# Windowed attention of a fused network on one Trainium2 core: in the last lane of a layer, the turn of a pair moved ahead of the values of the pair before it

## The reference, cut to what matters

```python
DIM, DEPTH, HEADS, DIM_HEAD, WINDOW = 128, 2, 8, 64, 64   # B, N = 2, 1024
def _layer(x, wqkv, qs, ksc, wo, lg, lb, w1, b1, w2, b2):
    h = shift_token(x)
    q, k, v = heads of h @ wqkv
    q, k = l2norm(q) * qs, l2norm(k) * ksc
    q, k = rotary_xpos(q, k)
    o = local_attention(q, k, v)      # each 64 tokens see themselves and the 64 before
    x = x + o @ wo
    h = layer_norm(shift_token(x)) * lg + lb
    a, g = split(h @ w1 + b1)
    return x + (a * gelu(g)) @ w2 + b2
```

## Time and profile before

| | |
|---|---|
| runs of the kernel | 2834.72, 2840.59, 2842.88 us, median 2840.59 |
| the profiled execution | 2833.55 us, its span 2831.8 us |
| mean granted clock of PE in it | 0.978 |
| busy share of the span | PE 94%, DVE 68%, ACT 66%, POOL 37% |
| windowed attention, last lanes | near 1920, 2153, 2522 and 2752 us of the span |

### The profile page before, as it was taken

One profiled execution on the slowest core, in us unless ns is written; L12 is line 12 of the kernel. 1 busy time (PEld: TensorE's weight loads), 2 busy tenths in 40 slices (PEclk: granted clock), 3 DMA queues, 4 the chain that ended last, 5 costly groups with the idle time before them and its releaser, 6 DMA issues.

```text
span 2831.8 us, 63348 instructions
## 1 busy us (share of the span) xinstructions
PE 2659.5 (94%) x24036; PEld 1812.7 (64%) x24036; DVE 1939.5 (68%) x5616; ACT 1858.8 (66%) x4392; POOL 1051.8 (37%) x876
## 2 busy tenths in 40 slices
PE   8999999999999998899999998998898998998998
PEld 5666656548888885588888885455455563553554
DVE  5555646488788786788888886774675326764774
ACT  5666766626676673478787876776776515875875
POOL 2323323313333330355555552553454013552551
PEclk8999999999999998999999999999999999999999
DMA  1010000000000001000000002210210002111210
GB/s 56 1 43 1 13 1 9 5 9 2 3 2 2 2 2 50 30 2 2 2 2 2 2 2 92 62 45 7 61 49 20 24 1 69 47 30 30 49 42 16
DMA packets 35280, 63.13 MB, mean 22 GB/s; under 512 B 11526, under 2 KB 15654, under 8 KB 33830
## 3 DMA queue, kind: packets, MB, share of 16 engines
q1 hardware_dynamic: 34982, 59.07, 7.5%
HBM read 23.48 MB, written 1.15 MB: 9 GB/s over the span
## 4 chain that ended last, share of the span: by engine, by line
PE 73%; DVE 11%; ACT 7%; issue 3%; SPq 2%; POOL 1%; DMA 1%; DVEq 0%; ACTq 0%; POOLq 0%
PE bank L804 63%; PE bank L1033 5%; PE bank L1153 3%; SPq L770 2%; PE bank L880 1%; ACT low L1364 1%; DVE low L1708 1%; DVE low L1686 1%; ACT work L1400 1%; ACT work L1303 1%; DVE halves L1701 1%; DMA work<-work 1%; DVE work L1588 1%; ACT squared L1275 1%; ACT bank L1279 1%
## 5 line engine op out<-in xcount | busy, mean ns | idle before, releaser
L1271 ACT ACTIVATE low<-bank 128x512 f32<-128x512 f32 (+3 forms) x512 | 427.8, 946 | 0.0
L804 PE MATMUL bank<-table_keys,halves 128*128 128x512 f32 (+3 forms) x1536 | 418.0, 380 | 1.1 <-ACT low L1364 1.0
L804 PE MATMUL bank<-work 128*64 128x128 f32 (+6 forms) x4480 | 364.2, 290 | 39.7 <-DVE work L1795 20.7
L804 PEld LDWEIGHTS bank<-work 128*64 128x64 f32 (+3 forms) x4480 | 265.0, 144 | 211.5 <-issue 147.5
L1364 ACT ACTIVATE low<-bank,low 128x512 f32<-128x512 f32 (+23 forms) x384 | 227.2, 592 | 248.9 <-DVE low L1708 245.4
L1708 DVE TENSOR_REDUCE low<-bank 128x1 f32<-128x512 f32 (+22 forms) x512 | 286.4, 569 | 96.2 <-PE bank L804 91.3
L1898 POOL TENSOR_TENSOR halves<-squared,const 128x512 fp32r<-128x512 f32 x128 | 137.0, 1070 | 510.7 <-PE bank L804 510.7
L1271 ACT ACTIVATE work<-bank 128x512 f32<-128x512 f32 (+4 forms) x389 | 199.5, 538 | 151.2 <-PE bank L804 76.9
L804 PEld LDWEIGHTS bank<-table_keys,halves 128*128 128x128 f32 x1536 | 243.6, 190 | 47.6 <-issue 13.3
L1400 ACT ACTIVATE work<-work 128x192 f32<-128x192 f32 (+1 forms) x512 | 218.7, 431 | 38.2 <-DVE work L1788 38.2
L1947 POOL TENSOR_TENSOR work<-work 128x768 f32<-128x768 f32 x128 | 187.7, 1466 | 135.2 <-DVE work L1799 135.2
(11 more groups left out here) (201 smaller groups left out, 5707.3 us busy)
## 6 DMA issues: line engine op xcount, KB each, us to landing
work<-work SPq DMA_DIRECT2D x512, 64.0 KB, 2.0
slot<-in_wW SPq DMA_DIRECT2D x4, 1605.5 KB, 6.7
slot<-in_wA SPq DMA_DIRECT2D x4, 837.0 KB, 6.4
table_low<-embv_padded SPq DMA_DIRECT2D x2, 1536.0 KB, 6.3
table<-in_dft SPq DMA_DIRECT2D x1, 3072.0 KB, 11.8
slot<-in_wE SPq DMA_DIRECT2D x2, 584.0 KB, 3.7
const<-in_const SPq DMA_DIRECT2D x1, 1094.5 KB, 5.2
squared<-in_x SPq DMA_DIRECT2D x4, 256.0 KB, 6.2
```

Source lines behind the costliest of these rows:

```text
L804: return pe.matmul(o, l, r, start=start, stop=stop)
L1271: return act.activation(dst, src, ACT.Identity)
```

## The change

In iterations of the last lane but its first, and after them (`turned`), the step `w_turn` of pair j - 1 is added behind `w_exps` and ahead of the values of pair j - 2, and not at its old place behind `w_weigh`. This holds for j = 25 to 31. Iteration 32 has `at` = 0 and keeps the old order (values 30, turn 31). Nothing else moves.

```diff
@@ -377,6 +377,10 @@
                     rotate(r)
                 if j < len(pairs):
                     add("w_exps", c=lane, i=i, hp=hp)
+                turned = (c >= C - 1 and at > 0)
+                if turned and j <= len(pairs):
+                    lane, i, hp = pairs[j - 1]
+                    add("w_turn", c=lane, i=i, hp=hp)
                 if 2 <= j <= len(pairs) + 1:
                     lane, i, hp = pairs[j - 2]
                     if i == 0:
@@ -393,7 +397,7 @@
                     add("w_weigh", c=lane, i=i, hp=hp)
                 if c + 1 < C and at in (3, 4, 5, 6):
                     add("w_value", c=c + 1, i=at - 3)
-                if 1 <= j <= len(pairs):
+                if not turned and 1 <= j <= len(pairs):
                     lane, i, hp = pairs[j - 1]
                     add("w_turn", c=lane, i=i, hp=hp)
                 if c and at == 2:
```

## The result

The changed kernel takes 2864.66 us (median of 5 runs, 2858.76 to 2867.73), the kernel before 2842.88 in the same comparison: ratio 1.0078, 95% interval 1.0053 to 1.0104, 21.8 us more. The forecast was 2856.5, 15.9 more, in a range of 2845 to 2868. The change is slower, for the reason forecast. Both medians lie above the sum of 15.9, and both intervals still hold it. In the profiled execution the schedule makes 17.2 us, and most of what it has beyond this is the clock.

A forecast was written before the change was run, and what follows sets the result against it. The prediction took latency, a chain of waits through several engines, to bound the last lanes. 2.35 + 0.81 + 0.81 = 3.97 us a lane, +15.9 in four, on the median 2840.59 gave 2856.5 us, range 2845 to 2868.

The forecast's parts named there:

- DVE's wait: On DVE, the turned tile's copy passes the next reciprocal, which then waits for PE's turn; reciprocal 25 at 2756.42, not 2754.95.
- Rival A: DVE's wait in iterations 25 and 26 is absorbed; only values 26 and 28 add, +6.5 us, 2847.1; chance 0.09.
- Rival B: Earlier copies remove PE's waits ahead of values 24, 26, 28: -7.0 us, 2830.9 with both clock falls gone; chance 0.05.
- Rival D: Engine order is not the plan's, so nothing moves: 2840.6 us; chance 0.03.
- Iterations 25 and 26: From turn 24 to lane 2's output product, reciprocal and turn 25 come later: +2.35 us a lane.
- Iterations 27 to 30: From scores 27 to scores 31, values 26 and 28 come onto the chain, 0.81 each: +1.6 us a lane.
- V26 0.81: Values 26 on PE, now between turn 27 and the norm's mean, adds 0.81 us from scores 27 to 29.
- Iteration 31 to V31: From scores 31 to values 31 at the lane's end: stays 8.21 us, 0 added; values 30 starts 0.3 us earlier.
- I keep two falls, as now: PE's clock falls to half in two of the four last lanes, as before, at 1.37 us each.
- a sign of being wrong: In the changed trace, a half clock showing in more than two last lanes would count against the forecast.
- Rival C: PE's clock falls in new gaps: every lane +2.7 us, 2859.2; one more in each +5.5, 2862.0; chance 0.13.

The follow-up runs named there:

- e1: The changed kernel with DVE back in the old order, new order kept on PE and ACT: 2852.79 us, 1.0045 of the kernel before.
- e9: The kernel before with the new order on DVE alone and 16 filler transposes ahead of values 30: 2837.28 us, 0.9971 of the kernel before.
- e4: The changed kernel with the change kept in iterations 27 to 31 alone: 2847.70 us, 1.0029 of the kernel before.
- e3: The changed kernel with the change kept in iterations 25 and 26 alone: 2846.74 us, 1.0030 of the kernel before.
- e8: The changed kernel run again, unaltered, on another chip: 2856.36 us against 2837.10 of the kernel before, 1.0066.
- e5: The changed kernel with PE's idle places filled by useless transposes of the identity: 2847.21 us, 1.0031 of the kernel before.
- e6: The kernel before with 18 useless transposes filling PE's gap ahead of values 30: 2831.28 us, 0.9976 of the kernel before.
- e7: The kernel before with the norm of lane 2 moved into PE's waits: 2821.19 us, 0.9933 of the kernel before.
- e11: The kernel before with 18 transposes ahead of values 30, repeated on another chip: 2829.12 us, 0.9944 of the kernel before.

## Why the prediction was right, and where its sum was short

*Direction and mechanism.* Right. DVE's wait: T24 at 2.58 us and its copy 0.91 us later, as forecast; the reciprocal behind it, the turn behind that. e1 takes the DVE half away and gets reciprocal 25 back, e9 has it alone. PE's half: S27 to S31 grows in e1 and e4 and not in e3 or e9. Rival A (the reciprocal keeps up) falls with the earlier trace rows against the DVE rows of after. Rival B (the copies free PE) too: the waits of 0.80 us ahead of V26 and V28 did go, and gave nothing, since T27 and T29 wait for POOL anyway. Rival D falls with the order of the rows.

*Iterations 25 and 26: +2.35 forecast, 2.21 measured* (8.31 - 6.10), and 2.31 up to S27. I had added the full lengths of copy and scaling, 0.69 and 0.68; back to back they start 0.61 and 0.60 apart. After it the product takes 3.63 us to S27 instead of 3.53.

*Iterations 27 to 30: +1.62 forecast, 1.99 to 2.00 measured.* The term "V26 0.81" was right, and its neighbours grew: T27 to V26 is 1.02 us, where a turn ahead of the 512-column matmuls of the norm took 0.93; the norm to S29 is 1.05, where it was 0.95. 0.19 a step, two steps.

*Iteration 31 to V31: 0 forecast; 0 at a full clock* (8.21 in the first lane of e8, 8.20 to 8.22 in e5). V30 starts 0.56 us earlier, where 0.3 was forecast, and gains nothing, since T31 waits for the multiply.

Together 4.30 us a lane and 17.2 in all against 3.97 and 15.9; between the two filled kernels the runs give 15.9. That this is the forecast's own number is luck, since those intervals reach over 3 us to either side. So is the match of e8's 2856.36 with the 2856.5: the kernel before stood 3.5 us lower there than the median that I added to.

*The clock: this is the term that failed.* "I keep two falls, as now", at 1.37 us each. The first profile after has a half clock in every last lane, which I had named as a sign of being wrong. In two of them there is a second, earlier fall, in T24, V23 and S26 of the second and in V26, the norm and S29 of the third. And a fall is dearer than the one I priced, because it lasts longer. Before, the granted clock was back by V31; now, in three of the four lanes, it stays at 0.50 through T31 and V31 and into the product. Windows behind T31 of the first lane before, and in the product of the fourth after (columns as in the earlier trace rows):

```profile
1953.40:1954.00 0.60, 0.00 (x0) 0.00 (x0) 0.60 (x1) 0.00 (x0) 0.00 (x0) 1.00 0.00 0
...
2818.00:2820.00 2.00, 2.00 (x3) 0.67 (x2) 0.00 (x0) 0.00 (x0) 0.00 (x0) 0.50 0.00 0
```

By windows of half a microsecond the first of these falls lasts from 1949.7 to 1953.2, some 3.4 us, and costs 1.37; the second from 2810.6 to 2820.9, 10.2 us, and costs 3.9 (45.54 against 41.65). The step that went wrong was to judge each new gap by itself, by V22 behind 1.45 us, and to price every fall by the shortest kind. What makes a fall long stays open: it isn't the shorter gap ahead of V30, since e1 and e3, whose gap there is 2.54 us as before, have falls of 10 us and more too.

Rival C had the direction and, for this profile, the count: six falls where there were two, one more a lane. Its price for one was too low by a factor of up to three. Between the medians of the runs, though, the clock adds only some 3.4 us (e5, e6, e8), less than C's 5.5, and that isn't clear of noise: the first profiled execution of the changed kernel was one of its slower ones, and e8's, at 2856.79 us, has three falls, in the second, third and fourth lane.

The Trainium skill ("TensorE: Matmul & The Clock Gate", Part 1) says that activity releases the throttle and that the point of the transition varies, because the activity is watched in a free-running way. The traces here agree: the filled kernels have no half clock in a last lane, and the two profiles of the changed kernel have six falls and three, at different places.

## What to carry to other kernels

Where a stretch is bound by a chain through several engines, ask of each piece whether it stands between two links or inside a wait: moving 0.81 us from a wait to between a turn and the next scores cost 0.99 to 1.01 us each time (e4), and moving 0.95 us the other way won 0.82 to 0.85 (e7), with PE's work unchanged. When a step is moved in a shared list, look at every engine's queue: a copy put ahead of a reciprocal made the reciprocal wait for PE. And waits on a matrix engine are priced twice, once as time and once as a clock that may fall behind them.

## What the runs showed of the hardware that I had not expected

Useless transposes in idle places of the kernel before made it faster by 0.24% (e6; on another chip by 0.56%, e11): 18 of them, 2.13 us of work ahead of V30, and the granted clock stays at full in all four lanes. The falls are of very different length and price: 3.4 us at half clock for 1.37 us from V30 on in the kernel before, 10.2 for 3.9 in the changed one, and in e3, whose lane ends in the old order, 5.25 us for one that lasts from V30 into the output product. So a count of falls doesn't price them. And the start-to-start distance of back-to-back matmul groups depends on the kind of the next group by some 0.1 us (T27 1.02 ahead of values, 0.93 ahead of the norm).
